# A graph network in one launch: attention in slots of four columns with a scan for the running maximum, and layer-norm stores issued by ScalarE

## Chip, cores and metric

One core of a Trainium2 chip. The metric is the device time of one execution in microseconds, here the median of three runs.

## The reference

50,000 nodes with 256 features and 50,000 edges sorted by destination, all in f32. Four graph layers follow each other, each added to its input and layer-normed:

```python
x = ln(x + gcn(x))      # two hops of h[dst] += norm * h[src], relu, @ W0.T + b0
x = ln(x + gat1(x))     # attention over edges, 8 heads of 32, edge attributes of 3
x = ln(x + gat2(x))     # attention over edges, 8 heads of 32, edge attributes of 64
x = ln(x + schnet(x))   # x[dst] * mlp(rbf) summed by src, an mlp, a batch norm, + x

# gat, per edge and head:
alpha = leaky_relu(a_src.h[src] + a_dst.h[dst] + edge_term, 0.2)
amax  = segment_max(alpha, dst)
ex    = exp(alpha - amax[dst])
out   = segment_sum(h[src] * ex / segment_sum(ex, dst)[dst], dst)
```

## The kernel before

The edges are laid out as 128 partitions by C = 392 columns: partition p holds edges p*392 to p*392+391 in order of destination, so that a segment runs along the columns of a partition. The nodes have the same layout. All phases work through the columns in slots of G = 2 columns (256 KB per tile of 256 features), 196 slots a phase, with NS = 4 buffers of each tile. The phases stand behind each other with a barrier between them: setup, hop_edges(0), hop_nodes, hop_edges(1), layer_nodes(0), attention_edges(1), layer_nodes(1), attention_edges(2), layer_nodes(2), filter_edges, update_nodes, finish_nodes. There is no planner: `unrolled(R, NS, [(stage, lag), ...])` writes out, for every engine by itself, step t as stage(t - lag) for each stage of its list, in the order of the list, and each engine carries out its instructions in that order. `hold(e, *done(stage, i, s, back))` makes an engine wait until `stage` has ended for the slot `back` slots earlier; back = NS is the wait for a buffer to be free.

`attention_edges(layer)` makes one pass with a running softmax. For each slot, SyncE loads edge attributes (`stage`, L896) and stores the running sums of the slot two steps back (`store`, L901). POOL gathers for each column the destination's row (L913) and the source's (L915), four indirect DMAs a slot, once `summed` of the slot NS back has ended. TensorE multiplies the attributes (L931); in layer 1 ACT applies the relu (L941). VectorE's list is `[(score, 0), (add, 1)]`: in `score` the logits of both columns (L977 to L985, in layer 2 L983 to L985), then column by column the running maximum in the last 8 words of the `sums` tile (L990, L991), where `pen` is 0 if the edge has the same destination as the one before and -1e30 if not, then the two differences for the exponentials (L992, L993), which ACT computes (L946). `add` belongs to the slot before: it weights the gathered rows (L1001), and for each column scales the running sum (L1008) and adds the row (L1010); then it signals `summed`.

`layer_nodes(layer)` gathers the finished sums (POOL, L717), loads x (SyncE, L688), adds and measures (VectorE), normalises (ACT, `ln_root` L626, `ln_apply` L642), and in layers 0 and 1 turns the result and multiplies it into the next layer's table (TensorE L831, L858; ACT copies it out, L801, L808, L810). SyncE's order in a step is: load(t), then store(t - APPLY - 2) of the normed rows (L696), then store_table(t - TABLE - 2) (L702 to L705). `finish_nodes` has the same pattern: load(t) of ht (L1346) and x (L1348), then store(t - 5) (L1352); ACT's list is batch_norm (L1379), ln_root, apply (L1386).

The lines on which SyncE's order rests, and VectorE's in attention:

```python
unrolled(R, NS, [(load, 0), (store, APPLY + 2)] + ([(store_table, TABLE + 2)] if table else []))   # layer_nodes
unrolled(R, NS, [(load, 0), (store, 5)])                                                           # finish_nodes
unrolled(R, NS, [(score, 0), (add, 1)])                                                            # attention
```

Of the kernel before, what the change touches and what calls it, by code (L numbers as in the profile page):

```python
# [62 lines left out]

def unrolled(rounds, slots, stages):

    for t in range(rounds * slots + max(lag for _, lag in stages)):
        for stage, lag in stages:
            if 0 <= t - lag < rounds * slots:
                stage((t - lag) // slots, (t - lag) % slots)


def build(nc, N, x, src, srcT, dst, dst_next, ew, rbfT, attr3T, attr64T, w0T, b0, w1T, w1, a1, encW, bias1,
# [50 lines left out]
    with ExitStack() as keep:  # L123
        def sb(name, shape, dt=F32):
            return keep.enter_context(sbuf(name, shape, dt))
# [6 lines left out]
        trash = sb("trash", [P, 1])  # L132
        ident, before, earlier, chain, chainT, penT = [sb(n, [P, P]) for n in ("ident", "before", "earlier", "chain", "chainT", "penT")]
# [10 lines left out]
        def setup():  # L144
            with ExitStack() as ctx:
# [42 lines left out]
                with nc.Block() as block:  # L188
# [33 lines left out]
                    def _(e):  # L222
# [17 lines left out]

                        link(e.memset(unit[:], 1.0))
# [38 lines left out]
                    def _(e):  # L280
                        e.wait_ge(prep, 12)
                        e.wait_ge(iotas, 12)
                        e.transpose(psT[:], firstf[:].to_broadcast([P, P]), ident[:]).then_inc(tr, 1)
                        e.wait_ge(prep, 15)
# [363 lines left out]
        def layer_nodes(layer):  # L648
# [4 lines left out]
            with ExitStack() as ctx:  # L653
# [26 lines left out]
                with nc.Block() as block:  # L680
                    @block.sync
                    def _(e):
# [10 lines left out]
                        def store(i, s):  # L693
                            c = bass.ds(i * (G * NS) + s * G, G)
                            hold(e, *done(st_["normed"], i, s))
                            e.dma_start(xout[:, c, :], xo[s][:]).then_inc(signal(stored, s), 16)  # L696

                        def store_table(i, s):
                            c = bass.ds(i * (G * NS) + s * G, G)
                            hold(e, *done(st_["evened"], i, s))  # L700
                            if layer == 0:
                                e.dma_start(nodes(T1)[:, c, :], tt[s][:]).then_inc(signal(stored_t, s), 16)  # L702
                            else:
                                e.dma_start(nodes(T2)[:, c, :], tt[s][:, :, 0:SW]).then_inc(signal(stored_t, s), 16)
                                e.dma_start(nodes(ET)[:, c, :], tt[s][:, :, SW:TW]).then_inc(signal(stored_t, s), 16)  # L705
# [761 lines left out]
```

## Time and profile before

| | |
|---|---|
| Runs (three) | 9191.78, 9195.85, 9219.41 us; median 9195.85 |
| Profiled execution | 9210.81 us, span 9209.1 us |
| Busy share of the span | VectorE 68%, POOL 59%, TensorE 52%, weight loads 37%, ACT 36% |
| DMA | 1839.84 MB, mean 200 GB/s |
| Mean granted TensorE clock | 0.718 of full speed |

The page gives the whole program; its shares are means over phases of very different kinds. The 40 slices of the page show them one behind the other, each 230 us long (digits are tenths):

```profile
PE   8856000039996333347771111100688887899743
DVE  7899333358887999977777777799544444455566
ACT  4433002347774111126660000144222222344588
POOL 7877777764445666655547777677788888100000
DMA  0299899989886445459984444588544444566688
```

Slices 13 to 17 are attention of layer 1, slices 22 to 25 mostly that of layer 2; layer_nodes(0) is in slices 9 to 12, layer_nodes(1) in 18 to 21, layer_nodes(2) in 26 to 28, and finish_nodes is in the last two or three.

### The profile page before, as it was taken

To read this page: it belongs to the slowest core of one execution; us is meant where nothing else is said; L and a number is where in the kernel's file an instruction comes from. 1 tells how busy PE (TensorE), PEld (TensorE's weight loads), DVE (VectorE), ACT (ScalarE), POOL (GpSimd) and SP (SyncE) were. 2 spreads that over 40 slices of the span, in tenths; PEclk is the share of its full clock that TensorE was granted. 3 is DMA by queue.
4 is the path that set the end of the run, shared out by engine and by line. 5 is a ranking of instruction groups with operands and counts; after the bars stand their busy time and mean duration, and the time that the engine had idled before them with its cause. 6 is when DMAs were issued, how large, how long until landed. Compare 5 with 4: busy or idle time off the path is not lost. (4 is left out here: it accounts for less than half of the span.)

```text
span 9209.1 us, 103278 instructions
## 1 busy us (share of the span) xinstructions
PE 4799.2 (52%) x18908; PEld 3452.2 (37%) x18908; DVE 6234.8 (68%) x20123; ACT 3278.4 (36%) x8442; POOL 5451.7 (59%) x5121
## 2 busy tenths in 40 slices
PE   8856000039996333347771111100688887899743
PEld 4422000038884211225551111100455555788622
DVE  7899333358887999977777777799544444455566
ACT  4433002347774111126660000144222222344588
POOL 7877777764445666655547777677788888100000
PEclk9999555569997555569995555555777778899855
DMA  0299899989886445459984444588544444566688
GB/s 20 99 344 338 284 309 297 309 274 299 297 294 195 146 146 148 147 173 285 278 268 117 122 122 123 165 266 266 108 79 79 79 79 79 165 200 199 214 292 284
DMA packets 1143019, 1839.84 MB, mean 200 GB/s; under 512 B 218094, under 2 KB 564898, under 8 KB 1142374
## 3 DMA queue, kind: packets, MB, share of 16 engines
q1 hardware_dynamic: 884838, 1245.79, 39.8%
q0 software_dynamic: 257536, 587.44, 26.3%
q14 instruction: 483, 3.96, 0.1%
q8 instruction: 162, 2.65, 0.1%
HBM read 1044.55 MB, written 788.03 MB: 199 GB/s over the span
## 5 line engine op out<-in xcount | busy, mean ns | idle before, releaser
L717 POOL DMA_INDIRECT st<-S,last_i x1176 | 1325.6, 1127 | 897.6 <-DVE yt L759 370.4
L915 POOL DMA_INDIRECT rows<-T,src_i x784 | 800.8, 1021 | 251.1 <-issue 248.1
L642 ACT ACTIVATE xo<-z,shift,rsd 128x256 f32<-128x256 f32 x1568 | 851.0, 591 | 1.3 <-issue 1.1
L1128 POOL DMA_INDIRECT A<-comb,ai x392 | 702.5, 1792 | 159.6 <-issue 145.0
L931 PE MATMUL psE<-encs,attr 4*128 4x256 f32 x784 | 404.9, 668 | 745.2 <-DMA attr<-in_attr3T 745.2
L946 ACT ACTIVATE ex<-diff 128x32 f32<-128x32 f32 x392 | 89.8, 229 | 1709.6 <-DVE diff L993 1709.6
L1200 DVE TENSOR_SCALAR eq<-psI,src_f 128x128 f32<-128x128 f32 x392 | 136.7, 349 | 743.2 <-DMA A<-comb,ai 708.4
L931 PE MATMUL psE<-fes,attr 64*128 64x8 f32 x784 | 199.5, 363 | 821.7 <-DMA attr<-in_attr64T 819.4
L477 DVE SCALAR_TENSOR_TENSOR sums<-sums,same,rows 128x256 f32<-128x256 f32 x784 | 380.2, 485 | 326.6 <-ACT rows L458 312.4
L1142 PE MATMUL psH<-rbf,wf1s 20*128 20x256 f32 x784 | 278.9, 485 | 613.9 <-DMA rbf<-in_rbfT 613.9
L931 PEld LDWEIGHTS psE<-encs,attr 4*128 4x128 f32 x784 | 227.5, 319 | 922.3 <-DMA attr<-in_attr3T 884.7
L613 DVE BATCH_NORM_STATS2 row_stats<-z 128x6 f32<-128x256 f32 x1568 | 560.6, 399 | 0.1
L913 POOL DMA_INDIRECT rowsd<-T,dst_i x392 | 384.1, 980 | 266.3 <-DVE sums L1010 150.3
L543 PE MATMUL psC<-sums,chain 128*128 128x256 f32 x4 | 2.4, 699 | 1034.9 <-PEq L417 1034.9
L1156 PE MATMUL psF<-wf2s,hid 128*128 128x256 f32 x1568 | 522.2, 494 | 0.0
L858 PE MATMUL psV<-w2s,xT 128*128 128x272 f32 x1568 | 436.5, 424 | 122.5 <-ACT tt L810 122.5
L931 PEld LDWEIGHTS psE<-fes,attr 64*128 64x128 f32 x784 | 181.2, 319 | 840.4 <-DMA attr<-in_attr64T 838.0
L458 ACT ACTIVATE rows<-rows,w_next 128x256 f32<-128x256 f32 x392 | 177.6, 500 | 850.8 <-DMA rows<-T,src_i 850.8
L445 POOL DMA_INDIRECT rows<-in_x,src_i x392 | 375.6, 958 | 170.0 <-issue 151.8
L1121 POOL DMA_INDIRECT rows<-X,dst_i x392 | 391.3, 998 | 135.9 <-issue 119.1
L913 POOL DMA_INDIRECT rowsd<-ET,dst_i x392 | 376.9, 962 | 150.3 <-issue 119.2
L445 POOL DMA_INDIRECT rows<-T,src_i x392 | 382.1, 975 | 127.7 <-issue 101.2
(232 smaller groups left out, 15612.8 us busy)
## 6 DMA issues: line engine op xcount, KB each, us to landing
X<-xo SPq DMA_DIRECT2D x588, 256.0 KB
xt<-X SPq DMA_DIRECT2D x588, 256.0 KB
S<-sums SPq DMA_DIRECT2D x392, 272.0 KB, 2.4
A<-zero SPq DMA_DIRECT2D x392, 256.0 KB, 4.8
S<-sums SPq DMA_DIRECT2D x392, 256.0 KB, 4.1
xt<-in_x SPq DMA_DIRECT2D x392, 256.0 KB
T<-tt SPq DMA_DIRECT2D x196, 280.0 KB
T<-tt SPq DMA_DIRECT2D x196, 272.0 KB
```

The source lines that it names most:

```text
L445: e.indirect_dma_start(rows[s][:, k, :], None, table, bass.IndirectOffsetOnAxis(ap=src_i[:, c:c + 1], axis=0))\
L477: ins = e.scalar_tensor_tensor(sums[s][:, k, 0:D], last, same[:, bass.ds(i * (G * NS) + (s * G + k), 1)], rows[s][:, k, :], ALU.mult, ALU.add)
L613: ins = e.bn_stats(row_stats[s][:, k, :], z[s][:, k, :])
L642: ins = e.activation(y[s][:, k, :], z[s][:, k, :], ACT.Identity, bias=shift[s][:, k, :], scale=rsd[s][:, k, :])
L717: e.indirect_dma_start(st[s][:, k, :], None, sums_table, bass.IndirectOffsetOnAxis(ap=last_i[:, c:c + 1], axis=0))\
L858: mm = e.matmul(psV[k][:, 0:DW], xT[s][:, k, m * P:(m + 1) * P], weights[:, m, :], start=m == 0, stop=m == K - 1)
L913: e.indirect_dma_start(rowsd[s][:, k, :], None, dtable, bass.IndirectOffsetOnAxis(ap=dst_i[:, c:c + 1], axis=0))\
L915: e.indirect_dma_start(rows[s][:, k, :], None, table, bass.IndirectOffsetOnAxis(ap=src_i[:, c:c + 1], axis=0))\
L931: mm = e.matmul(psE[s % 2][:, k * EW:(k + 1) * EW], attr[s][:, k, :], weights[:], start=True, stop=True)
L1121: e.indirect_dma_start(rows[s][:, k, :], None, X3, bass.IndirectOffsetOnAxis(ap=dst_i[:, c:c + 1], axis=0))\
L1128: e.indirect_dma_start(A[k], bass.IndirectOffsetOnAxis(ap=ai[s][:, k, :], axis=0), comb[s][:, k, :], None, compute_op=ALU.add).then_inc(si ...
L1156: mm = e.matmul(psF[s % 2][:, k * D:(k + 1) * D], hid[s][:, m, k * P:(k + 1) * P], wf2s[:, m, :], start=m == 0, stop=m == K - 1)
```

## The change

In attention, a slot holds four columns (QA = 4) and there are three buffers instead of four, hence 98 slots. The running maximum leaves the `sums` tile. It is computed by one `tensor_tensor_scan` over a tile of 8 heads by 5 entries: entry 0 of each head holds the maximum carried in from the slot before, entries 1 to 4 the logits; the scan computes state = max(state + penw, lg), and penw, a new table of 98 x 8 x 5 words made in setup (one memset and eight copies), is -1e30 in entry 0, so that a head starts anew, and the old `pen` in the others. ACT copies the maxima into the `sums` tile (`keep_max`), and the store waits for that as well. The rest of `score` and `add` does the same work in wider instructions; the scaling and adding stays column by column. As 98 is no multiple of 3, `written` and `total_of` take a count of slots. TensorE's waits on `prep` in setup are moved on by the nine new instructions.

In `layer_nodes` and `finish_nodes` the stores are issued by ACT, one step after the instruction that completes their tile, and SyncE's list is the load alone.

```diff
+        QA = 4
+        penw = sb("penw", [P, C // QA, H, QA + 1])
...
+                        link(e.memset(penw[:], NONE))
+                        for h in range(H):
+                            link(e.tensor_copy(penw[:, :, h, 1:QA + 1], pen[:].rearrange("p (t g) -> p t g", g=QA)))
...
# layer_nodes, SyncE (store and store_table go to ACT, word for word)
-                        unrolled(R, NS, [(load, 0), (store, APPLY + 2)] + ([(store_table, TABLE + 2)] if table else []))
-                        for sem, value in total(stored, R) + (total(stored_t, R) if table else []):
-                            e.wait_ge(sem, value)
+                        unrolled(R, NS, [(load, 0)])
...
# layer_nodes, ACT
-                        stages += [(lambda i, s: ln_root(e, i, s), ADD), (apply, APPLY)]
+                        stages += [(lambda i, s: ln_root(e, i, s), ADD), (apply, APPLY), (store, APPLY + 1)]
                         if table:
-                            stages += [(copy_turned_x, TURNX), (tabled_rows, TABLE)]
+                            stages += [(copy_turned_x, TURNX), (tabled_rows, TABLE), (store_table, TABLE + 1)]
...
# attention_edges
-                G, NS, LAG = 2, 4, 3
-                R = C // (G * NS)
+                G, NS = QA, 3
+                N = C // G
...
+                lg, mx = [[ctx.enter_context(sbuf(f"{n}{s}", [P, H, G + 1], F32)) for s in range(NS)] for n in ("lg", "mx")]
...
+                mp = [ctx.enter_context(sbuf(f"mp{s}", [P, H, G], F32)) for s in range(NS)]
+                diff, ex = [[ctx.enter_context(sbuf(f"{n}{s}", [P, 2, H, G], F32)) for s in range(NS)] for n in ("diff", "ex")]
...
                             hold(e, *done(summed, i, s))
+                            hold(e, *done(maxed, i, s))
                             e.dma_start(nodes(S)[:, c, :], sums[s][:]).then_inc(signal(stored, s), 16)
...
-                            e.activation(enc[s][:].rearrange("p g d -> p (g d)"), psE[s % 2][:], ACT.Relu).then_inc(signal(rectified, s), 1)
+                            for k in range(0, G, 2):
+                                ins = e.activation(enc[s][:, k:k + 2, :].rearrange("p g d -> p (g d)"),
+                                                   psE[(i * NS + s) % 2][:, k * EW:(k + 2) * EW], ACT.Relu)
+                            ins.then_inc(signal(rectified, s), 1)
...
+                        def keep_max(i, s):
+                            hold(e, *done(scored, i, s))
+                            hold(e, *done(stored, i, s, NS))
+                            e.copy(sums[s][:, :, VW:SW], mx[s][:, :, 1:G + 1].rearrange("p h g -> p g h")).then_inc(signal(maxed, s), 1)
...
-                            link(e.scalar_tensor_tensor(lg[s][:], dot[s][:], 0.2, dot[s][:], ALU.mult, ALU.max))
-
-                            for k in range(G):
-                                pc = pen[:, bass.ds(i * (G * NS) + (s * G + k), 1)]
-                                last = sums[s][:, k - 1, VW:SW] if k else sums[(s - 1) % NS][:, G - 1, VW:SW]
-                                e.tensor_scalar(mp[s][:, k, :], last, pc, None, ALU.add)
-                                link(e.scalar_tensor_tensor(sums[s][:, k, VW:SW], last, pc, lg[s][:, k, :], ALU.add, ALU.max))
-                            link(e.tensor_tensor(diff[s][:, :, 0:H], mp[s][:], sums[s][:, :, VW:SW], ALU.subtract))
-                            e.tensor_tensor(diff[s][:, :, H:2 * H], lg[s][:], sums[s][:, :, VW:SW], ALU.subtract).then_inc(signal(scored, s), 1)
+                            by_column = lambda a: a.rearrange("p h g -> p g h")
+                            flat = lambda a: a.rearrange("p h g -> p (h g)")
+                            e.tensor_copy(lg[s][:, :, 0], mx[(s - 1) % NS][:, :, G])
+                            link(e.scalar_tensor_tensor(by_column(lg[s][:, :, 1:G + 1]), dot[s][:], 0.2, dot[s][:], ALU.mult, ALU.max))
+                            pw = penw[:, i * NS + s, :, :]
+                            link(e.tensor_tensor_scan(flat(mx[s][:]), flat(pw), flat(lg[s][:]), 0.0, ALU.add, ALU.max))
+                            e.tensor_tensor(mp[s][:], mx[s][:, :, 0:G], pw[:, :, 1:G + 1], ALU.add)
+                            link(e.tensor_tensor(diff[s][:, 1, :, :], lg[s][:, :, 1:G + 1], mx[s][:, :, 1:G + 1], ALU.subtract))
+                            e.tensor_tensor(diff[s][:, 0, :, :], mp[s][:], mx[s][:, :, 1:G + 1], ALU.subtract).then_inc(signal(scored, s), 1)
...
-                        unrolled(R, NS, [(score, 0), (add, 1)])
+                        written(N, NS, [(score, 0), (add, 1)])
...
# finish_nodes, SyncE and ACT
-                        unrolled(R, NS, [(load, 0), (store, 5)])
+                        unrolled(R, NS, [(load, 0)])
...
-                        unrolled(R, NS, [(batch_norm, 0), (lambda i, s: ln_root(e, i, s), 2), (apply, 3)])
+                        unrolled(R, NS, [(batch_norm, 0), (lambda i, s: ln_root(e, i, s), 2), (apply, 3), (store, 4)])
```

## Rows read from the trace of the kernel before

**Rows 1.** Busy times of three stretches: first hop, attention of layers 1, 2

```profile
core 0: us, PE busy (x) PEld busy (x) DVE busy (x) ACT busy (x) POOL busy (x), PEclk, DMA share, GB/s
392.00:935.00 543.00, 319.01 (x786) 137.12 (x786) 490.80 (x1576) 177.79 (x392) 377.80 (x394) 0.97 0.98 332
2878.90:4032.30 1153.40, 404.86 (x784) 227.50 (x784) 1043.83 (x3143) 163.03 (x393) 785.21 (x784) 0.50 0.50 146
4838.20:5864.00 1025.80, 199.49 (x784) 181.17 (x784) 758.01 (x2748) 46.20 (x197) 776.60 (x784) 0.50 0.41 121
```

**Rows 2.** The same view, 100 us each of layer_nodes(0), (1), (2), finish_nodes

```profile
2256.00:2356.00 100.00, 99.80 (x536) 84.97 (x536) 85.56 (x268) 76.64 (x224) 48.88 (x45) 1.00 0.90 298
4400.00:4500.00 100.00, 70.86 (x303) 50.57 (x303) 76.13 (x281) 65.57 (x203) 55.17 (x51) 0.95 0.91 279
6100.00:6200.00 100.00, 0.00 (x0) 0.00 (x0) 98.29 (x368) 43.19 (x100) 79.38 (x67) 0.50 0.87 268
8900.00:9000.00 100.00, 40.66 (x148) 25.87 (x147) 62.42 (x257) 81.74 (x185) 0.00 (x0) 0.50 0.89 291
```

**Rows 3.** Timeline of a slot in attention 1: start, duration, engine, line, tile

```profile
3300.22 0.43 DVE L1010 TENSOR_TENSOR sums<-sums,rows 128x264 f32<-128x264 f32 x1
3300.69 0.69 DVE L977 TENSOR_TENSOR enc<-enc,rowsd 128x512 f32<-128x512 f32 x1
...
3301.20 0.25 SPq L896 DMA_DIRECT2D attr<-in_attr3T  x1
...
3301.44 0.94 POOL L913 DMA_INDIRECT rowsd<-T,dst_i  x1 [0.91 <-DVE sums L1010]
...
3302.76 0.23 DVE L990 TENSOR_SCALAR mp<-sums,pen 128x8 f32<-128x8 f32 x1
...
3303.36 2.07 PE L931 MATMUL psE<-encs,attr 4*128 4x256 f32 x4 [3.68 <-DMA attr<-in_attr3T]
...
3303.97 0.70 DVE L1001 TENSOR_TENSOR rows<-rows,ex 128x528 f32<-128x528 f32 x1
...
3305.64 0.60 ACT L941 ACTIVATE enc<-psE 128x512 f32<-128x512 f32 x1 [1.15 <-PE psE L931]
...
3306.46 0.69 DVE L977 TENSOR_TENSOR enc<-enc,rowsd 128x512 f32<-128x512 f32 x1
```

**Rows 4.** Timeline of attention 2: a slot's last gather, and its reader

```profile
5149.68 0.95 POOL L915 DMA_INDIRECT rows<-T,src_i  x1 [0.30 <-issue]
...
5152.55 0.18 DVE L983 TENSOR_TENSOR dot<-rows,rowsd 128x16 f32<-128x16 f32 x1 [0.40 <-DMA rows<-T,src_i]
```

**Rows 5.** A product of 1024 elements in the timeline; the scan's line (min/median/max)

```profile
4040.64 1.22 DVE L1076 TENSOR_TENSOR mall<-mall,mn 128x1024 f32<-128x1024 f32 x1
...
L378 DVE TENSOR_TENSOR_SCAN number<-unit,psNum x1: 970/970/970, 386.6 to 386.6; 128x392 f32<-128x392 f32 x1
```

**Rows 6.** Who waited for whom in layer_nodes(1): us, times, longest

```profile
DVE xb L728 <- DMA xt<-X: 173.5, 132, 3.9
...
SPq L108 <- ACT tt L810: 196.4, 193, 2.8
```

**Rows 7.** Timeline of a slot in finish_nodes

```profile
8903.42 0.34 SPq L1352 DMA_DIRECT2D out<-xo  x1
...
8904.50 1.09 ACT L1379 ACTIVATE ht<-ht,shift,scale 128x256 f32<-128x256 f32 x2 [1.17 <-DMA xt<-X]
8904.52 0.52 SPq L1348 DMA_DIRECT2D xt<-X  x1
8905.50 0.28 ACT L626 ACTIVATE sd<-mean_var,epsc 128x2 f32<-128x2 f32 x1
...
8905.68 1.08 ACT L642 ACTIVATE xo<-z,shift,rsd 128x256 f32<-128x256 f32 x2
```

**Rows 8.** Setup's shapes: groups by line, busy us and mean ns

```profile
L467 DVE MEMSET sums<- 128x512 f32 x4 | 1.9, 485 | 1.4 <-PEq L1413 1.2
...
L237 DVE TENSOR_TENSOR same<-dst_f 128x391 f32<-128x391 f32 x1 | 0.6, 566 | 0.0
...
L239 DVE TENSOR_SCALAR pen<-same 128x392 f32<-128x392 f32 x1 | 0.4, 364 | 0.0
```

More of the change, by code:

```diff
@@ L61, in total, with total_of, written @@
     return [(sem, rounds * (16 * dmas if dmas else slots)) for sem in sems]
+def total_of(stage, count):
+    sems, slots, dmas = stage
+    return [(sem, len(range(s, count, slots)) * 16 * dmas) if dmas else (sem, count) for s, sem in enumerate(sems)]
+def written(count, slots, stages):
+    for t in range(count + max(lag for _, lag in stages)):
+        for stage, lag in stages:
+            if 0 <= t - lag < count:
+                stage((t - lag) // slots, (t - lag) % slots)
 def unrolled(rounds, slots, stages):
[L66 to L69, printed above, removed]
+    written(rounds * slots, slots, stages)
 def build(nc, N, x, src, srcT, dst, dst_next, ew, rbfT, attr3T, attr64T, w0T, b0, w1T, w1, a1, encW, bias1,
@@ L893, in stage @@
                         def stage(i, s):
[L894 removed]
+                            c = bass.ds((i * NS + s) * G, G)
                             hold(e, *done(encoded, i, s, NS))
@@ L916, in gather @@
                                     .then_inc(signal(gathered, s), 16)
-                        unrolled(R, NS, [(gather, 0)])
+                        written(N, NS, [(gather, 0)])
                     @block.tensor
@@ L952, in _ @@
                         for s in range(NS):
+                            e.memset(mx[s][:], 0.0)
                             ins = e.memset(sums[s][:], 0.0)
@@ L957, in _ @@
                         e.wait_ge(started, 1)
-                        SC = 8 if layer == 1 else 6
+                        SC = 7 if layer == 1 else 5
                         def score(i, s):
@@ L1016, in add @@
                             hold(e, *done(summed, i, s))
-                        unrolled(R, NS, [(score, 0), (add, 1)])
+                        written(N, NS, [(score, 0), (add, 1)])
                 with nc.Block() as block:
-                    end = sums[NS - 1][:, G - 1, :]
+                    end = sums[(N - 1) % NS][:, G - 1, :]
                     t = lambda n, sh: ctx.enter_context(sbuf(n, sh, F32))
@@ L1384, in apply, with store @@
                             ln_apply(e, i, s, finished)
-                        unrolled(R, NS, [(batch_norm, 0), (lambda i, s: ln_root(e, i, s), 2), (apply, 3)])
+                        def store(i, s):
+                            hold(e, *done(finished, i, s))
+                            e.dma_start(out[:, bass.ds(i * (G * NS) + s * G, G), :], xo[s][:]).then_inc(signal(stored, s), 16)
+                        unrolled(R, NS, [(batch_norm, 0), (lambda i, s: ln_root(e, i, s), 2), (apply, 3), (store, 4)])
+                        for sem, value in total(stored, R):
+                            e.wait_ge(sem, value)
                     @block.vector
```

62 lines of the change are left out of this document (29 added, 33 removed).

## The prediction

> **What bounds the kernel now.** The kernel is a row of phases with a barrier behind each, so I read it phase by phase: first the busy times of the stretches, then one period of the timeline in each phase that the diff touches, then who waits for whom. No engine bounds the whole.
>
> Attention of layer 1 takes 1153.4 us, of layer 2 1025.8 us [rows 1]. In layer 2 POOL issues 784 gathers in a busy 776.6 us, 0.99 each, and the gap behind each is 0.30; 784 x 1.29 is 1011 of the 1026 us. That phase is bound by the issuing of gathers, not by their bytes (DMA share 0.41). In layer 1 the gathers are as many and as long (785.2 us), but a slot of two columns comes only every 5.77 us where POOL alone would need 4 x 1.30 = 5.2. The period in [rows 3] shows why: VectorE starts slot after slot back to back (L977 at 3300.69 and again at 3306.46), and POOL's first gather of a slot sits idle 0.91 us until VectorE has released its buffer. VectorE sets the pace there. A second chain is just as long: the attribute load goes out at 3301.20, held until the add that ended at 3300.65, the matmuls start at 3303.36, ACT's relu at 3305.64, VectorE at 3306.46. It must shrink with the rest or it becomes the bound.
>
> Of the phases with layer norms, layer 0 has a slot every 4.44 us (45 gathers of 2 per slot in 100 us) with TensorE 99.8% busy: bound by TensorE. Layer 2 has one every 2.99 us with VectorE 98.3% busy. Layer 1 (3.90 us a slot) and the last phase (148 transposes, 4 per slot: 2.70 us) have no full engine; the DMA share is 0.91 and 0.89 [rows 2]. What comes last in them is a load: VectorE waited 173.5 us for xt in layer 1, while SyncE, which issues it, waited 196.4 us for ACT's table rows before a store that stands ahead of that load [rows 6]. In the last phase the load of ht and xt goes out at 8904.52 only because the store of an earlier slot in front of it was held to 8903.42; ACT then starts at 8904.50 after 1.17 us of idling for an xt [rows 7].
>
> **Setup.** Added ahead of everything: a memset of 3920 elements and eight strided copies of 392, each chained. A memset of 512 took 485 ns, so 3.7 us at the same rate; a pass over 392 took 0.36 us with one input and 0.57 with two [rows 8], with a gap of 0.04, so 3.2 to 4.9 us. VectorE's chain is what setup waits for: nothing covers it. +7.5 us, between 6.5 and 9.
>
> **Attention, layer 1.** Per four columns the old score work is 2 x 3.28 (L977 to L1001), the old add 2 x 2.49 (L1001 to the next L977) [rows 3]: 11.54 us. The new score: product and reduction over 1024 elements, each at the 1.22 of a product of that size [rows 5] and its gap, 2.50; two small adds 0.44 (from L977 to L990 lie 2.07 us, 1.44 for the two large ones at 512 elements and 0.21 for each of three small ones); the copy of the last maximum 0.14, as for an instruction that waits for nothing; leaky relu 0.22; the scan over 40 elements; three more, 0.46. The scan of 392 took 970 ns [rows 5]. By proportion 40 cost 0.10, and at most 0.30 as for a small instruction twice over; I take 0.28 with its gap. Sum 4.05. The column-by-column chain of four instructions and two subtractions, 1.21 us from L990 to L1001 for two columns, was the dear part. The new add: eight column instructions as before, at 0.465 each, and the wide product over 1056 instead of 528, 0.63 + 0.55: 4.90. VectorE's slot is 8.95 us for four columns, down from 11.54.
>
> VectorE then isn't last any more. POOL alone: 8 x 1.30 = 10.4 us. But there are three slots now, and a gather of slot t+3 waits for the add of slot t, which VectorE runs behind the score of slot t+1, and that waits for all gathers of t+1. Around that ring lie 10.1 us of gathers (8 x 1.00 + 7 x 0.30), the landing, the score, the add and the release. Landing: the last gather of a slot ended at 5150.63 and VectorE started at 5152.55 [rows 4], 1.92 us, taken as 1.95. Release: add ended at 3300.65, gather began at 3301.44, 0.79 [rows 3]. 10.1 + 1.95 + 4.05 + 4.90 + 0.79 = 21.8 us for two slots: 10.9 a slot, just over POOL's own 10.4. So the new bound is a ring of POOL, landing and VectorE. 97 x 10.9 = 1057, and behind the last slot's first gather 10.1 + 1.95 + 4.05 + 2 x 4.90 = 25.9: 1083 us against 1153, or -70. The same reckoning gives the phase before as 1142 (196 slots and 11 at the ends) where 1153 were measured; such small stalls will not all go, so I take -65. Bounds: -118 if the ring is shorter and POOL alone counts; -15 if landing takes 3 us, since every microsecond in the ring costs 49.
>
> The second chain: 0.55 to the load's issue, 2.2 to land, four matmul pairs 4.1, two relus 1.2, three handovers 0.5: 8.5 us, under 10.9. The matmuls would wait for the store, the relus for exp and the new copy of the maxima, both small (0.2 each) on an ACT that is busy 163 of 1153 us [rows 1]. The store now waits for that copy as well, which ends before the add: no cost.
>
> **Attention, layer 2.** Score 1.55, ring 10.1 + 1.95 + 1.55 + 4.90 + 0.79 = 19.3, 9.65 a slot, under POOL's 8 x 1.29 = 10.3. Nothing saved. Behind the last gather lie two adds of 4.9 instead of 2.5: +4.8; the last store of twice the size, some 0.6 in each layer. +6 for both.
>
> **Stores on ACT.** SyncE is left with loads, whose waits are four slots back. Issuing cost SyncE 0.34 us for a store and 0.52 for a load [rows 7]; ACT pays at least nothing (the issue runs while its data path works through the two normalisations queued before it) and at most 0.34 to 0.52 plus the waits. I take nothing in the likeliest case: the root at 8905.50 and the normalisations at 8905.68 [rows 7] follow their predecessors without a gap although waits stand between them, so its front part works ahead. The cover is 1.08 us of work per slot at L642; gone, it costs as in the third rival. The Trainium skill, page Advanced Engine Details and Errata, section Sequencer Loop, says as much: other engine instructions can be queued while a control instruction runs. No row of before shows it for a DMA on ACT.
> Layer 0: TensorE stays full: 0. Layer 2: VectorE stays full: -3. Layer 1: loads go out earlier, the wait for xt goes, and the DMA engines are next. The highest share in the trace is 0.98 [rows 1]; 3.90 x 0.91/0.98 = 3.62, 196 x 0.28 = 55 us at best, nothing at worst; I take -35. Last phase: 2.70 x 0.89/0.98 = 2.45, ACT's own 81.74/37 = 2.21 is under it: 49 at best; I take -30. Two thirds of each, since layer 0 with full queues stands at 0.90 as a phase bound elsewhere, which shows no ceiling but no proof of 0.98 with these stores either.
>
> **Sum.** 7.5 - 65 + 6 - 35 - 3 - 30 = -119.5. The profiled execution took 9210.8 us (span 9209.1), giving 9091; the median of the runs is 9195.85, 15 lower, and I state the time against it: 9076.
>
> **Rivals.**
> 1. The stores move and the node phases keep their time: 0.9 is what the DMA engines give with reads and writes mixed (three phases stand at 0.87 to 0.91). For it: these shares are alike. Against: 0.98 at 332 GB/s in the first hop. 7.5 - 65 + 6 = -51: 9145. The Trainium skill, page DMA: Bandwidth & Descriptors, section Issuing engines are not separate DMA queues, would have it so: issuing from several engines only saves the time to initiate. The row of SyncE's wait speaks for a gain from order, not from bandwidth. Chance 0.25.
> 2. The ring in attention is longer or shorter than I took. With landing at 3 us, -15 instead of -65: 9126, chance 0.10. With POOL alone and the DMA at 0.98: 7.5 - 113 + 6 - 104 - 3 = -206: 8990, chance 0.10. For it: VectorE's terms are sums of small gaps.
> 3. Slower: ACT pays for the issues in full. It has 4.44 - 3.41 us free for two in layer 0, 3.90 - 2.57 for three in layer 1, 2.70 - 2.21 for one at the end. Up to 0.44 each nothing is lost; at 0.60 with waits layer 1 gives 4.37 (+92), layer 0 4.61 (+33), the end 2.81 (+22): +147 - 51 = +96, 9292. It decides from about 0.52. Against: the cover above. Chance 0.06.
> 4. The change does not do what it says, in that the attribute chain stays the pace in layer 1: it would need over 10.9 where I find 8.5. 9140, chance 0.04.
>
> **Numbers.** Forecast 0.45, rivals as above. The forecast's own range is 9040 to 9110; with the first rival and the landing one 9010 to 9165, leaving out the 8990 case and the slower one. Within 0.3% (28 us) is about what a measurement of this kernel cannot tell from no change: 0.05. Faster 0.89, slower 0.06.
>
> **What would show it.** Attention 1 about 1088 us, gathers of a slot 10.9 apart with about half a microsecond of POOL idle and VectorE waiting for landings, not ACT; attention 2 about 1031 with POOL gap after gap of 0.30; scan near 0.24 us. Node phase 1 near 3.7 us a slot and the last near 2.55, with shares over 0.93, SyncE waiting on slots four back. It is wrong if POOL waits over 1 us a slot, if ACT shows gaps of the size of an issue behind L642, or if the share stays at 0.9.

## The result and the profile after

The changed kernel takes 9052.4 us (median of four runs, 9048.41 to 9054.36) beside 9193.82 us for the kernel before (four runs). The ratio of the runs is 0.9841, with a 95% interval of 0.9821 to 0.986. The profiled execution has a span of 9052.2 us against 9209.1.

The total came out 24 us under the forecast, but not by the way that was forecast. The table shows both traces phase by phase, from the first gather (or first load) of a phase to that of the next, with the two halves of the change run by themselves. "nodes 0" stands for layer_nodes(0), "attention 1" for attention_edges(1), and so on; the last two columns are filter_edges with update_nodes, and finish_nodes:

| us | up to layer_nodes(0) | nodes 0 | attention 1 | nodes 1 | attention 2 | nodes 2 | filter, update | finish |
|---|---|---|---|---|---|---|---|---|
| before | 1965.9 | 913.1 | 1176.9 | 784.2 | 1046.6 | 606.9 | 2169.8 | 545.7 |
| after | 1970.2 | 897.6 | 1185.1 | 661.0 | 1116.9 | 592.5 | 2176.3 | 452.6 |
| stores_only | 1963.6 | 898.0 | 1173.9 | 661.9 | 1045.9 | 595.2 | 2170.8 | 454.7 |
| attention_only | 1969.0 | 921.3 | 1185.5 | 772.7 | 1117.6 | 606.9 | 2171.4 | 546.5 |

The node phases gave 246 us where 68 were forecast; attention lost 78 where 59 were to be gained. The windows of after that answer to [rows 1, 2], in their order (the two attentions, then 100 us each of layer_nodes(0), (1), (2) and finish_nodes):

```profile
core 0: us, PE busy (x) PEld busy (x) DVE busy (x) ACT busy (x) POOL busy (x), PEclk, DMA share, GB/s
2867.80:4029.00 1161.20, 369.31 (x784) 244.01 (x784) 831.32 (x1870) 147.76 (x393) 841.52 (x784) 0.50 0.48 144
4713.90:5808.00 1094.10, 183.29 (x784) 174.21 (x784) 586.16 (x1671) 43.96 (x197) 839.14 (x784) 0.50 0.38 113
2256.00:2356.00 100.00, 100.00 (x543) 86.16 (x542) 86.59 (x268) 78.06 (x229) 56.68 (x45) 1.00 0.92 301
4400.00:4500.00 100.00, 77.38 (x370) 58.93 (x369) 92.57 (x339) 80.35 (x247) 74.30 (x62) 1.00 1.03 337
6100.00:6200.00 100.00, 0.00 (x0) 0.00 (x0) 99.79 (x379) 44.36 (x104) 78.25 (x68) 0.50 0.91 274
8800.00:8900.00 100.00, 49.74 (x180) 32.08 (x180) 76.29 (x314) 97.55 (x226) 0.00 (x0) 0.50 1.01 354
```

Three things stand in them. VectorE is relieved in both attentions as worked out (1043.8 to 831.3 us busy in layer 1, 758.0 to 586.2 in layer 2) and the phases get no shorter. POOL's busy time for the same 784 gathers rises from 785.2 to 841.5 and from 776.6 to 839.1 us: a gather costs 1.07 us where it cost 1.00 and 0.99. And the slots of layer_nodes(1) come every 3.2 us (62 gathers in 100 us, two a slot) instead of 3.90, those of the last phase every 2.2 (180 transposes, four a slot) instead of 2.70, at a DMA share above 1.

Where the gathers lose time shows in the timeline of attention 2 (start, duration, engine, line):

```profile
5299.85 1.25 DVE L1029 TENSOR_TENSOR rows<-rows,ex 128x1056 f32<-128x1056 f32 x1
5300.11 1.81 POOL L934 DMA_INDIRECT rows<-T,src_i  x1 [0.30 <-issue]
...
5310.97 1.25 DVE L1029 TENSOR_TENSOR rows<-rows,ex 128x1056 f32<-128x1056 f32 x1
5311.15 1.91 POOL L934 DMA_INDIRECT rows<-T,src_i  x1 [0.30 <-issue]
```

One gather in each slot begins just after the weighting of the rows has begun. The first ends at 5301.92, 0.82 us after VectorE's product ended at 5301.10; the second at 5313.06, again 0.84 after 5312.22. A gather alone takes 0.95. POOL is the bound here, and the slot is 11.1 us long in both rows, so that a gather is hit in slot after slot: in the 98 slots of this phase 95 gathers began under L1029, and they took 1.80 us on average.

### The profile page after: what moved, and what is told of

Same layout as the page of the kernel before. It is cut to its first block and busy times, and to the rows that moved or that the text cites. A ratio compares the mean times of both kernels' runs of the same rounds, so it can differ in the third digit from the quotient of the medians.

```text
span 9052.2 us, 99177 instructions
## 1 busy us (share of the span) xinstructions
PE 4690.6 (52%) x18908; PEld 3454.8 (38%) x18908; DVE 5861.7 (65%) x17783; ACT 3257.5 (36%) x8442; POOL 5656.9 (62%) x5121
## 5 line engine op out<-in xcount | busy, mean ns | idle before, releaser
L716 POOL DMA_INDIRECT st<-S,last_i x1176 | 1417.3, 1205 | 652.4 <-issue 315.6
L934 POOL DMA_INDIRECT rows<-T,src_i x784 | 883.3, 1127 | 246.4 <-issue 237.3
L950 PE MATMUL psE<-encs,attr 4*128 4x256 f32 x784 | 369.3, 649 | 775.7 <-DMA attr<-in_attr3T 775.7
L968 ACT ACTIVATE ex<-diff 128x64 f32<-128x64 f32 x196 | 50.2, 256 | 1962.6 <-DVE diff L1021 1962.5
L932 POOL DMA_INDIRECT rowsd<-T,dst_i x392 | 419.2, 1069 | 223.4 <-issue 96.9
L873 PE MATMUL psV<-w2s,xT 128*128 128x272 f32 x1568 | 407.6, 403 | 137.7 <-ACT tt L809 137.7
L1149 POOL DMA_INDIRECT rows<-X,dst_i x392 | 390.9, 997 | 135.2 <-issue 119.1
L460 POOL DMA_INDIRECT rows<-T,src_i x392 | 380.1, 970 | 126.5 <-issue 98.2
```

The lines of the kernel that those rows point to most:

```text
L460: e.indirect_dma_start(rows[s][:, k, :], None, table, bass.IndirectOffsetOnAxis(ap=src_i[:, c:c + 1], axis=0))\
L716: e.indirect_dma_start(st[s][:, k, :], None, sums_table, bass.IndirectOffsetOnAxis(ap=last_i[:, c:c + 1], axis=0))\
L873: mm = e.matmul(psV[k][:, 0:DW], xT[s][:, k, m * P:(m + 1) * P], weights[:, m, :], start=m == 0, stop=m == K - 1)
L932: e.indirect_dma_start(rowsd[s][:, k, :], None, dtable, bass.IndirectOffsetOnAxis(ap=dst_i[:, c:c + 1], axis=0))\
L934: e.indirect_dma_start(rows[s][:, k, :], None, table, bass.IndirectOffsetOnAxis(ap=src_i[:, c:c + 1], axis=0))\
L950: mm = e.matmul(psE[(i * NS + s) % 2][:, k * EW:(k + 1) * EW], attr[s][:, k, :], weights[:], start=True, stop=True)
```

## The experiments

The first four kernels ran on one chip (the kernel before 9211.27 us there), the next four on a second (9540.15), the last four on a third (9584.2). On the second and third the phases up to layer_nodes(0), nodes 1 and attention 2 are longer in every kernel, so that only ratios, and phases of runs on one chip, are compared. The changed kernel itself was run on neither of these two.

### The two halves

```diff
# stores_only: the kernel before, with layer_nodes and finish_nodes of the change
# attention_only: the changed kernel, with layer_nodes and finish_nodes of before
```

> The kernel before with the stores of layer_nodes and finish_nodes issued by ACT, and nothing else. Theory: the whole gain is here and the attention of before is untouched. From the phases of the two traces (layer_nodes(0) -15, (1) -123, (2) -14, finish_nodes -93) about 8950 us, faster than the changed kernel. Rival: the phases gain only together, and attention's share of the gain is real: then this kernel stays above the 9052 of the changed one.

> The changed kernel with its stores back on SyncE, so the attention change and the table in setup alone. Theory: attention 1 +8 us, attention 2 +70, setup +5 to +7, so about 9280. Rival (my prediction's step: attention 1 loses 65, attention 2 +6): about 9145.

stores_only: 8961.22 us, 0.9731 (0.9715 to 0.9748). attention_only: 9284.91 us, 1.0081 (1.0063 to 1.01). The spans differ from before by -245.1 and +81.8, together -163; the whole change by -157. The halves add up, phase by phase as in the table. All of the gain is in the stores; the attention and its table make the kernel slower, by 0.8%, more than its interval allows for.

### The stores: which order, or which engine

```diff
# later_stores: the kernel before, all issued by SyncE as before
-unrolled(R, NS, [(load, 0), (store, APPLY + 2)] + ([(store_table, TABLE + 2)] if table else []))
+unrolled(R, NS, [(load, 0), (store, APPLY + 3)] + ([(store_table, TABLE + 3)] if table else []))
...
-unrolled(R, NS, [(load, 0), (store, 5)])
+unrolled(R, NS, [(load, 0), (store, 6)])
```

> The kernel before, all stores still on SyncE, but those of layer_nodes and finish_nodes written one step later in its list, so that each load stands one slot further ahead of the store it used to queue behind. Theory order (the loads were held by the store's wait): most of the gain comes with one queue too, layer_nodes(1) falls from 784 us to 670-720 and finish_nodes from 546 to 460-500, the whole some 110 to 180 us under the kernel before. Theory second queue (the gain is from ACT's own queue or its issue): both phases stay within 10 us.

9308.05 us, 0.976 (0.9738 to 0.9783). Its nodes 1 took 690.2 us and its last phase 450.0; the three kernels of the same chip that have ACT issue the stores took 674 to 681 and 452 to 456. With one issuing engine the DMA engines are as full, and move 316 and 351 GB/s where the changed kernel has 337 and 354 in its 100 us (columns as above):

```profile
4250.00:4900.00 650.00, 489.84 (x2294) 374.24 (x2292) 559.80 (x2063) 476.32 (x1526) 414.98 (x367) 0.99 0.98 316
...
8860.00:9290.00 430.00, 216.31 (x777) 138.94 (x778) 330.79 (x1356) 419.15 (x967) 0.00 (x0) 0.50 1.00 351
```

So what cost the time before was a store whose data weren't ready yet standing ahead of the next load. One step of distance removes that as well as a second engine does, but for 9 to 16 us in layer_nodes(1), which these runs don't explain.

### The attention: a wait in the ring, or the gathers themselves

```diff
# four_buffers: the changed kernel
-                G, NS = QA, 3
+                G, NS = QA, 4
```

> The changed kernel with four buffers in attention instead of three. Theory A (POOL's gathers, lengthened by VectorE, bound attention 2; in attention 1 POOL also idles 84 us for buffers): attention 1 loses some 70 us, attention 2 keeps its 1117: about 8985. Theory C (the ring of three buffers costs both): both fall, by 70 and by 60, about 8925.

8950.61 us, 0.9721 (0.9705 to 0.9737). Attention 1 falls from 1185.1 to 1094.3 us, attention 2 hardly, from 1116.9 to 1109.1. The score's product (L1005) now starts evenly, 10.8 us apart, where it came 13.56 and 9.33 apart with three buffers:

```profile
3310.84 1.23 DVE L1005 TENSOR_TENSOR enc<-enc,rowsd 128x1024 f32<-128x1024 f32 x1 [1.87 <-DMA rows<-T,src_i]
...
3321.62 1.23 DVE L1005 TENSOR_TENSOR enc<-enc,rowsd 128x1024 f32<-128x1024 f32 x1 [1.85 <-DMA rows<-T,src_i]
```

The ring of three buffers was the bound in layer 1 and is gone; what is left there is POOL's own pace with these gathers (eight of 1.04 us on average and a gap of 0.30 behind each: 10.7 us a slot). In layer 2 the ring wasn't the bound. The total lies between the 8985 and the 8925 that were expected of the two theories, and the phases go with theory A.

```diff
# split_wide: the changed kernel, still three buffers
-                                link(e.tensor_tensor(e4, e4, hd, ALU.mult))
+                                for k in range(G - 1):
+                                    e.tensor_tensor(e4[:, k], e4[:, k], hd[:, k], ALU.mult)
+                                link(e.tensor_tensor(e4[:, G - 1], e4[:, G - 1], hd[:, G - 1], ALU.mult))
...
-                            e.tensor_tensor(v, v, wide(...), ALU.mult)
+                            for k in range(G):
+                                e.tensor_tensor(v[:, k], v[:, k], ex[s][:, 1, :, k:k + 1].to_broadcast([P, H, HW]), ALU.mult)
```

> The changed kernel with its two widest two-input VectorE instructions (the product in score, the weighting in add) cut into four of one column each. Theory A, a gather that begins while VectorE runs an instruction with two SBUF inputs waits for its end, so its delay grows with the instruction's length: the mean gather falls from 1.07 to about 1.00 us, attention 2 from 1117 to about 1050 and attention 1 from 1185 to about 1130, the whole near 8940. Theory B, the gathers are long for another reason (bytes in flight, three buffers): no change but the three extra instructions of each, within 15 us of 9052 or slower.

9012.43 us, 0.9791 (0.9775 to 0.9808). The same product lies over 1.46 us, but in four pieces, and a gather is held up by one piece at most:

```profile
5201.97 1.46 DVE L1032 TENSOR_TENSOR rows<-rows,ex 128x264 f32<-128x264 f32 x4
5202.39 1.17 POOL L934 DMA_INDIRECT rows<-T,src_i  x1 [0.30 <-issue]
...
2861.00:4030.00 1169.00, 371.28 (x792) 245.47 (x792) 868.52 (x2460) 147.80 (x393) 798.41 (x785) 0.50 0.48 144
4707.00:5780.00 1073.00, 185.25 (x792) 175.85 (x792) 610.62 (x1972) 44.12 (x198) 799.66 (x785) 0.50 0.40 116
```

In layer 2 POOL is busy 39.5 us less than in after, and the phase is 30.6 us shorter although VectorE has more to do. So the long gathers are a cost of that phase, and cutting the products gives back 30.6 of the 70.3 us that it had lost; the gathers still take 23 us more than in the kernel before. In layer 1 POOL's busy time falls by 43 us too, but the phase stays at 1186.8: with three buffers it waits for VectorE instead (119.1 us for buffers, 81.8 in after), whose slot got longer. The expectation (1050, 1130 and a total of 8940) was right in the direction for layer 2, with less than half the size, and wrong for layer 1.

### What makes a gather longer: two inputs, or a busy VectorE

```diff
# extra_two: the changed kernel, in layer 2 ahead of the weighting; both write a spare tile
+                                e.tensor_tensor(spare (viewed as v), v, wide(...), ALU.mult)
# extra_one: the same place, the same 1056 elements, one input
+                                e.tensor_reduce(spare[:, :, 0], zero[:, 0:VW] broadcast over g, AX, ALU.add)
```

> The changed kernel with one more VectorE instruction a slot in attention 2, ahead of the weighting in add: the same product of 1056 elements with two SBUF inputs, written to a spare tile. VectorE waits 466 us for landings there, so its time alone is covered. Theory A (a gather waits for the two-input instruction under which it begins): the gathers grow again and attention 2 goes from 1117 us to about 1160 (1135 to 1215). Theory B (long gathers for another reason): attention 2 within 10 us.

> The same place and about the same duration, but a reduction over 1056 elements with one SBUF input. Theory A: no gather waits for it, attention 2 stays within 10 us of 1117. Theory B', that any long VectorE instruction lengthens a gather: as with the two-input one.

9282.85 us (0.9731) and 9294.03 us (0.9743), one round each, attention 2 1158.1 and 1164.0 us. The extra instruction lasts 1.25 us in both. First extra_one, where L1031 has one input, then extra_two, where it has two:

```profile
5404.41 1.25 DVE L1031 TENSOR_REDUCE spare<-zero 128x4 f32<-128x1056 f32 x1
5404.54 0.95 POOL L935 DMA_INDIRECT rows<-T,src_i  x1 [0.30 <-issue]
5405.57 1.25 DVE L1032 TENSOR_TENSOR rows<-rows,ex 128x1056 f32<-128x1056 f32 x1
5405.79 1.85 POOL L933 DMA_INDIRECT rowsd<-ET,dst_i  x1 [0.30 <-issue]
```

```profile
5417.33 1.25 DVE L1031 TENSOR_TENSOR spare<-rows,ex 128x1056 f32<-128x1056 f32 x1
5417.50 1.90 POOL L935 DMA_INDIRECT rows<-T,src_i  x1 [0.30 <-issue]
5418.50 1.25 DVE L1032 TENSOR_TENSOR rows<-rows,ex 128x1056 f32<-128x1056 f32 x1
```

The gather of 5404.54 lies wholly under the reduction and takes 0.95; that of 5405.79 begins under the product and ends 0.82 after it. Over the whole phase 81 gathers began under the reduction, and none took over 0.95 us; under the product that stands in its place in extra_two 93 began, and they took 1.28 to 2.00. So a busy VectorE alone doesn't lengthen a gather.

The two instructions differ in more than their inputs, though: the reduction writes 4 words and the product 1056. The kernel before parts these two. Its L779 adds 512 elements and writes 512 in 0.68 us in every layer, but in layer_nodes(0) one operand comes from PSUM, in layers 1 and 2 both come from SBUF:

```profile
2512.05 0.68 DVE L779 TENSOR_TENSOR z<-psZ,xb 128x512 f32<-128x512 f32 x1
2512.28 0.95 POOL L717 DMA_INDIRECT st<-S,last_i  x1 [0.30 <-issue]
...
6062.84 0.68 DVE L779 TENSOR_TENSOR z<-z,xb 128x512 f32<-128x512 f32 x1
6063.07 1.27 POOL L717 DMA_INDIRECT st<-S,last_i  x1 [0.30 <-issue]
```

Both gathers begin 0.23 us into the sum. The first takes 0.95, the second ends 0.82 after the sum. Of the gathers that begin with more than 0.2 us of L779 left, all 20 beside the PSUM operand take 0.95; of 254 beside two SBUF operands 245 end 0.82 us after it. The other nine began within 0.03 us of the sum's start and took 0.95, and the sum lasted 0.73 to 0.75 us instead: there the gather came first. The cause of the length is a VectorE instruction that reads two operands from SBUF.

The pair doesn't show its price in time. The two phases differ by 6 us in the wrong direction: the gathers of the phase take 854 us in extra_two and 824 in extra_one, but POOL's stops for buffers, over the usual gap of 0.30, come to 26 and 62 us. extra_one missed its expectation (within 10 us of 1117) most likely for a reason of the chip (below): POOL's 62 us of stops have no counterpart in after, whose attention 2 has 2.5. The price rests on split_wide.

### The landing of gathers beside the store

```diff
# double_store: the changed kernel; S2 is a second table of the size of S
                             e.dma_start(nodes(S)[:, c, :], sums[s][:]).then_inc(signal(stored, s), 16)
+                            e.dma_start(nodes(S2)[:, c, :], sums[s][:]).then_inc(signal(stored, s), 16)
```

> The changed kernel, where attention stores each slot's sums twice (a second tensor that nothing reads), 544 KB more per slot. Theory landing (the store that goes out at the end of an add delays the landing of the slot's last gather, and that delay lies in the ring of three buffers): attention 1 grows by 40 to 80 us from 1185, attention 2, where POOL sets the pace, by under 15. Rival (the ring's excess is VectorE's and POOL's alone): attention 1 within 10 us.

9336.62 us, 0.9787 (0.9759 to 0.9816), one round. Attention 1 takes 1229.0 us against 1188.3 and 1188.4 in the two kernels above, which do the same there but for the second store; attention 2 1172.4 against 1158.1 and 1164.0. VectorE's waits for landings in layer 1 are 313 us against 273 to 275. In its trace the last gather of a slot ends at 3527.04 and the score follows at 3530.67, 3.63 us later:

```profile
3524.81 0.32 SPq L921 DMA_DIRECT2D S<-sums  x1
...
3525.18 0.43 SPq L922 DMA_DIRECT2D S<-sums  x1
...
3526.09 0.95 POOL L936 DMA_INDIRECT rows<-T,src_i  x1 [0.30 <-issue]
...
3530.67 1.22 DVE L1007 TENSOR_TENSOR enc<-enc,rowsd 128x1024 f32<-128x1024 f32 x1 [6.03 <-DMA rows<-T,src_i]
```

In every other slot the landing stands in the ring of three buffers. There it takes 3.49 us on average (from the last gather's end to the score) against 2.60 in the two kernels above; 48 turns of 0.89 are 43 us, the 41 that the phase grew. So the store is in the ring of layer 1, through the landing of the gathers beside it.

### The scan by itself, and a kernel of the best parts

```diff
# scan_two: the changed kernel with slots of two columns and four buffers
-        QA = 4
+        QA = 2
...
-                G, NS = QA, 3
+                G, NS = QA, 4
# mix: four_buffers in layer 1, the attention of before in layer 2
# mix_split: mix, with the wide products of both cut by column as in split_wide
# stores_again: stores_only once more
```

> The stores on ACT and the scan, but slots of two columns and four buffers as before (196 slots, head tables of 3 entries). It parts the scan from the wider slot. Per slot the old running maximum took 1.21 us (L990 to L1001) and the relu 0.2; the copy 0.14, the relu 0.22, the scan 0.26 and three small instructions 0.5 make 1.12: the slot of VectorE falls from 5.73 to 5.4 us. The chain from the end of an add through the store, the attribute load behind it, the matmuls and the relu to the score two slots on takes 5.65 us and is shared out over two slots with VectorE's own 5.4: (5.65 + 5.4) / 2 = 5.5. Theory (wide instructions are what the change gains by and what it pays for in layer 2): attention 1 near 196 x 5.5 + 11 = 1090 us, attention 2 as before, 1046 within 5, because the products stay at 528 elements; total near 0.964 to 0.968 of the kernel before. Rival A (attribute chain alone sets the pace with slots of two columns): attention 1 stays at 1174, ratio 0.974. Rival B (the scan itself, not the width, costs layer 2 its 70 us): attention 2 over 1080, ratio 0.968 or more in spite of a faster layer 1.

> The stores on ACT; in layer 1 the new attention with four buffers, in layer 2 the attention of before. Composition of the phases measured so far: attention 1 1094 us, attention 2 1046, the rest as with the stores alone: 8950.6 - 63 = 8887 on a chip where before takes 9211, a ratio of 0.965. If the phases influence each other (by what is left in the queues at the barrier) it is off this by more than 15 us.

> As mix, and the products of 1024 and 1056 elements in layer 1 each cut into four by column, those of 528 in layer 2 into two. Port theory (a gather that begins while VectorE runs an instruction with two inputs in SBUF lasts until 0.82 us after it ends): a piece lasts 0.35 us, so no gather lasts over 1.2 us, the mean falls from about 1.08 to 1.01 in layer 1, and with POOL as the bound there (four buffers) 784 x 0.06 = 45 us go; in layer 2 0.99 to 0.97, POOL bound, 12 us. Ratio near 0.959 to 0.961. Rival (the number of instructions on VectorE counts: in layer 1 it is busy over 0.9, and six more instructions of some 0.06 us fixed cost make its slot 0.4 us longer, 98 x 0.4 = 39 us): no better than mix, 0.965 or above.

> The kernel before with its layer-norm stores on ACT and nothing else, again, to stand beside the three others on the same chip. Every theory: ratio 0.973 as before. If scan_two, mix and mix_split lie under it, the attention's gain in layer 1 can be had without the loss in layer 2; if they lie at it, the loss is not in the width.

| | us | ratio | attention 1 | attention 2 |
|---|---|---|---|---|
| scan_two | 9382.83 | 0.9785 (0.9767 to 0.9802) | 1217.0 | 1216.3 |
| mix | 9386.45 | 0.9793 (0.9776 to 0.981) | 1210.3 | 1214.2 |
| mix_split | 9377.34 | 0.9776 (0.9758 to 0.9794) | 1213.9 | 1211.6 |
| stores_again | 9368.9 | 0.977 (0.9753 to 0.9787) | 1195.4 | 1218.9 |

mix was expected at 0.965 and mix_split at 0.96; both are at stores_again or a little above it. scan_two was expected at 0.964 to 0.968 and isn't there either. Attention 2 is the same within 8 us in four kernels with three kinds of code for it, and attention 1 no better than with the old code: on this chip something else sets the pace of both. The same kernel on two chips shows how much: from stores_only to stores_again the time up to layer_nodes(0) grows by 192 us, attention 1 by 22, nodes 1 by 21 and attention 2 by 173, the other phases by 3 us or less each. The traces show it. In 200 us of attention 2 of the kernel before a gather follows the last by 0.30 us without exception, 1.295 us from one to the next. On the second and third, besides the same 0.30, POOL stands still for some 1 to 6 us every 24 to 36 us in most kernels (in 200 us of attention 2 on the third chip the gathers come 1.47 to 1.56 us apart), and VectorE halts between two instructions of one chain. Of later_stores, first who waited for whom, then its attention 2:

```profile
DVE mp L990 <- remote: 32.4, 18, 2.4
...
5463.74 0.23 DVE L990 TENSOR_SCALAR mp<-sums,pen 128x8 f32<-128x8 f32 x1 [2.44 <-issue]
5465.23 0.95 POOL L915 DMA_INDIRECT rows<-T,src_i  x1 [0.30 <-issue]
...
5471.54 0.94 POOL L913 DMA_INDIRECT rowsd<-ET,dst_i  x1 [5.37 <-DVE sums L1010]
```

The last row says what POOL stood still for: VectorE's add, which had not yet released the buffer. Such stops come to 139 us in this attention 2. So in these rows the halts begin in VectorE's chain, where they end with "remote" or with nothing that the trace names, and POOL's stops follow from them. No wait of the first chip's traces has "remote" as its end. What the halts are isn't settled by these runs. For scan_two one thing can be read beside them: its VectorE slot is short (from L1005 at 3508.51 to L1029 at 3511.29, 2.78 us where [rows 3] have 3.28), and then VectorE waits for the chain of attributes:

```profile
3511.72 2.07 PE L950 MATMUL psE<-encs,attr 4*128 4x256 f32 x4 [4.15 <-issue]
...
3514.00 0.60 ACT L961 ACTIVATE enc<-psE 128x512 f32<-128x512 f32 x1 [2.02 <-issue]
...
3514.72 0.69 DVE L1005 TENSOR_TENSOR enc<-enc,rowsd 128x512 f32<-128x512 f32 x1 [0.99 <-issue]
```

That speaks for its rival A, that with two columns the attribute chain takes over; attention 2 within 3 us of stores_again speaks against rival B. Neither is more than that on this chip. Whether mix gives its 0.965 on the first chip wasn't run: there, stores_only (8961.22) and four_buffers (8950.61) are the fastest kernels measured, both better than after, and not told apart from each other by their intervals.

## Why the prediction was right in the sum and wrong in its steps

That the sum fits is luck. The node phases gave 178 us more than forecast and attention cost 137 us more, two errors with different causes and opposite signs. The signs that the text named show it: slots of attention 1 come 11.7 us apart where it said 10.9, and slots of layer_nodes(1) 3.2 where it said 3.7.

**Setup.** +7.5 forecast; the memset took 3.33 us and the copies 0.37 each, 6.6 in all with their gaps, and the first load of the first hop was issued 6.8 us later than before (398.0 us against 391.2). Two hops on, the table shows 4.3 of that. Right.

**VectorE's slot.** Right in every term: from L1005 at 3299.97 to L1029 at 3304.04 lie 4.07 us (4.05 forecast), the scan takes 0.24, and from a score's start to the gather that its add releases lie 9.72 (4.05 + 4.90 + 0.79 = 9.74). The chain that bounded the kernel before was read rightly.

**The ring of layer 1.** The mechanism was right, its size was not. The rows of after, with the gathers that wait for a buffer and the scores that wait for a landing:

```profile
3298.94 0.94 POOL L932 DMA_INDIRECT rowsd<-T,dst_i  x1 [0.91 <-DVE sums L1038]
...
3309.07 0.34 SPq L920 DMA_DIRECT2D S<-sums  x1
3309.10 0.95 POOL L934 DMA_INDIRECT rows<-T,src_i  x1 [0.30 <-DVE sums L1038]
...
3313.53 1.23 DVE L1005 TENSOR_TENSOR enc<-enc,rowsd 128x1024 f32<-128x1024 f32 x1 [4.63 <-DMA rows<-T,src_i]
...
3323.25 1.65 POOL L932 DMA_INDIRECT rowsd<-T,dst_i  x1 [2.31 <-DVE sums L1038]
...
3333.22 0.94 POOL L934 DMA_INDIRECT rows<-T,src_i  x1 [0.30 <-issue]
...
3336.36 1.23 DVE L1005 TENSOR_TENSOR enc<-enc,rowsd 128x1024 f32<-128x1024 f32 x1 [4.56 <-DMA rows<-T,src_i]
...
3346.07 0.94 POOL L932 DMA_INDIRECT rowsd<-T,dst_i  x1 [0.90 <-DVE sums L1038]
```

The forecast was 10.1 + 1.95 + 8.95 + 0.79 = 21.8 us for two slots. The first turn, from 3298.94, took 11.11 for eight gathers, 3.48 for the landing (3310.05 to 3313.53) and 9.72 for VectorE and the release: 24.3. The second took 10.91 + 2.20 + 9.71 = 22.8. Over the whole phase a turn takes 11.09 + 2.60 + 9.72 = 23.4 us on average, 1.6 more than forecast, and 48 turns of that are 78 us: the distance between the 1083 us that it reckoned and the 1161.2 measured. Two terms failed. "8 x 1.00" took the duration of a gather from a kernel whose products are half as wide: 1.0 us a turn. "1.95" took the landing from layer 2 with small stores, though the text itself priced 3 us as a bound: 0.65 a turn. The landing goes by when the store is issued: in the 23 slots of this phase whose last gather begins 0.03 us behind the store, as at 3309.10, it takes 2.86 to 3.49 us, in the 25 where it begins about 1 us behind 2.02 to 2.52, and in the 47 where the store is 10 us or more away 1.86 to 2.04. four_buffers, split_wide and double_store show ring, gathers and landing in turn. Taken together, both terms leave nothing of the gain, and the prediction had moved only one of them.

**Layer 2.** The step "Nothing saved" was right and "+6" missed the same term: 784 gathers took 62.5 us more, of 70.3 us that the phase grew; another 5 lie behind the last gather, as forecast (4.8). This cost was in no bound, for the prediction asked of every engine what it waits for and never whether two of them disturb each other while both work. The trace of before had it: a gather there took 0.99 us on average where one alone takes 0.94 [rows 1, 3], and the 216 that begin under L1001 in the two attentions take 1.12 on average and up to 1.43. A product twice as long holds up whatever begins under it for up to 0.55 us more. The Trainium skill, page Advanced Engine Details and Errata, section Miscellaneous Facts (GPSIMD Details), says that Pool shares a read and a write interface with DVE and conflicts with DVE instructions that have two SBUF inputs. By that rule every wide product beside the gathers is a suspect; extra_two and extra_one (1.90 and 0.95 us) and the two kinds of L779 (1.27 and 0.95) agree with it. The page SBUF — State Buffer, in the Trainium skill, section Who interferes with whom, says that a VectorE instruction with two SBUF inputs contends with a GpSimd instruction that reads SBUF, but also that a tensor_tensor was not seen to stall a DMA. For these indirect gathers, whose offsets lie in SBUF, the rows agree with the first (1.81 and 1.91 us beside L1029) and not with the second, and the measurement decides.

**Stores on ACT, hidden.** Right. The issues lie under the data path's work; in the last phase ACT is at 97.55% with them and loses nothing:

```profile
8851.29 1.09 ACT L1401 ACTIVATE ht<-ht,shift,scale 128x256 f32<-128x256 f32 x2
...
8851.92 0.34 ACTq L1410 DMA_DIRECT2D out<-xo  x1
...
8852.47 1.08 ACT L657 ACTIVATE xo<-z,shift,rsd 128x256 f32<-128x256 f32 x2
8853.45 1.08 ACT L1401 ACTIVATE ht<-ht,shift,scale 128x256 f32<-128x256 f32 x2
```

The store is issued at 8851.92 while ACT's own instruction of 8851.29 still runs, and the period of 2.16 us has no gap between ACT's instructions. The loads alone now make SyncE wait for buffers, 534 us for L765 in layer_nodes(1), in place of the table rows of [rows 6].

**What that gives.** Here the size failed: -68 forecast, -246 measured (-15.5, -123, -14, -93). The step was "3.90 x 0.91/0.98" and its fellow for the last phase: a slot can shrink by no more than the DMA share lacks to 0.98, and then two thirds of that for caution. But the share isn't the part of a fixed ceiling in use. layer_nodes(1) went from 279 to 337 GB/s while its share went from 0.91 to 1.03, the last phase from 291 to 354 with 0.89 to 1.01; both moved more bytes than the 332 GB/s of [rows 1] that served as the ceiling. The last phase stops at ACT's own 2.2 us a slot, a bound that the prediction had written down (2.21) and then not used, because 2.45 seemed to come first. Layers 0 and 2 stayed near their bounds (TensorE, VectorE) and still gave 15 us each; that these were small stalls behind late loads is likely but not shown.

**The rivals.** The first, that 0.9 is all that the DMA engines give, is refuted by 1.03. Its page of the Trainium skill, DMA: Bandwidth & Descriptors, section Issuing engines are not separate DMA queues, says that issuing from several engines saves only the time to initiate; later_stores agrees that a second issuer isn't needed; what it shows besides is that the order of stores and loads in one engine is worth 2.4%. The second had its landing half come true in part (2.60 us on average where it stands in the ring, not 3) and its other half in the node phases. The third, ACT paying in full, and the fourth, the attribute chain, did not occur in after; scan_two shows where the fourth would have.

## What to carry to other kernels

Read a queue for what stands ahead of a load: a store issued before its data are ready delays every load behind it, and one step more of distance gave 2.4% of the whole kernel here. When an instruction is made wider, ask what runs beside it: a gather that begins under a product of two SBUF operands waits for its end, so half as many products, each twice as wide, can lengthen a phase bound by gathers. An operand from PSUM, or a single SBUF input, doesn't hold it up. In a ring of few buffers, price each term by what it will be in the new kernel (wider stores, longer gathers); four buffers instead of three took 91 us off attention 1.

## What the runs showed of the hardware

- An indirect DMA on POOL takes 0.95 us of issue, or until 0.82 us after the end of a product or sum of two SBUF operands on VectorE that runs when it begins: up to 2.03 us beside a product of 1.25. A reduction of the same length (81 gathers) and a sum with one operand in PSUM (20) leave it at 0.95. If it begins within 0.03 us of the sum's start, it goes first and the sum lasts some 0.06 us longer (9 gathers).
- A gather landed 1.86 to 2.04 us after its end with no store of 544 KB issued in the 10 us before it, and 2.86 to 3.49 after it with one issued 0.03 us before it; with two such stores it took 3.49 on average.
- The DMA share of these traces reaches 1.03; two phases at 0.89 and 0.91 still took on 21% more bytes a second.
- Issuing a store (0.34 us) cost ACT nothing measurable while its data path had work, even at 97.55% busy.
- The same kernel took 9211, 9540 and 9584 us on three chips, the difference lying in phases full of gathers, with halts whose end the trace names "remote" or not at all. On the third chip the savings in attention vanished. What a change in such a phase is worth has to be measured on more than one chip.
